# Moving ScalarE's weight casts and slice stores, and one VectorE shift, in a hand-ordered attention block

## The chip, the cores and the metric

The program runs on one core of a Trainium2 chip. The metric is the device time of one execution in microseconds (us). It is compared as the median of several executions; the kernel before had 2206.11 us as the median of three (2204.46 to 2212.1).

## What is computed

A two-layer block on 64 sequences of 32 tokens with 512 features (2048 tokens), all in float32. Only the first layer's attention is touched by the change:

```python
x = x + L0_attn(L0_cond(x, ...), wq, wkv, wo)     # 32 heads of 128, softmax over 32 keys, causal
x = x + L0_ffn(L0_cond2(x, ...), ...)
x = x + L1_attn(L1_cond(x, ...), ...)
x = x + L1_ffn(L1_cond2(x, ...), ...)

# L0_attn
q = einsum('bsd,de->bse', h, wq);  k, v = the two halves of einsum('bsd,de->bse', h, wkv)
probs = softmax(where(causal, q @ k.T * scale, -1e30))
return einsum('bse,ed->bsd', probs @ v, wo)
```

## The kernel before

The first layer's attention is one block of the program (function `attention`), from about 88 to 1686 us of the profiled span. Every engine has its own list of instructions there, written out by hand, and the lists meet only in semaphores. No scheduler decides anything: the order in the source is the order on each engine.

**Bodies and slots.** The 2048 tokens are two pairs of tiles of 512 tokens (`pair` 0 and 1), and the 32 heads are eight groups of four. One `body(it, pair, ...)` does four heads for one pair of tiles; there are sixteen of them, `it` 0 to 7 for pair 0 and 8 to 15 for pair 1. A body is six slots `s`. Slots 0, 1, 4 and 5 make queries and keys (`qk`) of one head each, slots 2 and 3 the values (`v_tok`) of all four. Each slot's product of weights and input is done with seven smaller products instead of eight (`product`, names P1 to P7), where weights and inputs were combined by sums first. Each float32 product is three TensorE matmuls on a high and a low part (`mm3`, lines 215 to 217).

**Weights.** `HeadWeights` prepares the seven combined weight blocks `j` of a slot. ScalarE writes the high part (`high`, line 984: a cast), GpSimd forms the four sums (`sums`: lines 997, 1000, 1003 and 1007) and subtracts for the low part (`low`, line 1018). The weights of a slot are called H0, H1, V (slots 2 and 3 together), H2 and H3. The high part `(1,)` has to wait for GpSimd's second sum (line 1000), and GpSimd's first sum (line 997) writes to a place that TensorE's product P5 of the slot before still reads:

```python
if j in SUM_OF:
    act.wait_ge(self.sum_done, w * 4 + (SUM_OF[j] + 1))
act.activation(self.part(kind, j, 0), src, ACT.Copy).then_inc(self.hi_done, 1)
```

**Copies.** In a slot, three products leave PSUM by ScalarE's `copy_chain(it, s, k)` (line 1250; k = 0, 1, 2 behind P6, P5 and P3), one by `keep_p1` (line 1242), and three by VectorE's `mix(it, s, k)` (line 1421; behind P2, P7 and P4). TensorE's P5 waits for `copy_chain(.., 0)`, and its P3 for `copy_chain(.., 1)`.

**Softmax and output.** `scores` (line 1708) is followed on VectorE by `soft_shift` (lines 1438, 1443, 1444), on ScalarE by `exps` (line 1255), on VectorE by `soft_divide` (1451 to 1453) and `soft_turn` (1459, four transposes of 32x32 blocks). `prob_times_v` (line 1719) is followed by ScalarE's `o_high` (line 1260, two casts of 128x512 to `o_hi`) and VectorE's `o_low` (line 1465, two subtractions to `o_lo`). Then `output(T, m)`, four times six matmuls with `wo`, waits in its first call for both low parts:

```python
if m == 0:
    pe.wait_ge(wo_ready, ow + 1)
    pe.wait_ge(tail_free, T * 6 + 5)
```

The results are added to the residual by VectorE's `add_out` (line 1471).

**Slices for the second pair.** During pair 0, VectorE's `part(j)` (lines 1401, 1406, 1408) forms a slice of the combined inputs of the second half of the tokens in `stage`, and ScalarE's `store(j)` (line 1236) sends it to DRAM by DMA. `stage` is one buffer, so each `part` waits until the store before has landed. In pair 1 `store` and `part` do nothing. `out_high` (line 1273) casts the 128x1024 output weights.

Of the kernel before, what the change touches and what calls it, by code (L numbers as in the profile page):

```python
# [1050 lines left out]
def attention(nc, t, sb, sem, overlaid, const, consts, mm3, resid, psum, kept_raw, kept, hw, v_tok, combos, later, ahead):  # L1051
# [7 lines left out]
    with ctx:  # L1059
# [172 lines left out]
        @block.scalar  # L1232
        def _(act):
            def store_part(it, j):
                wait_apart(act, part_step, parts_done(it, PART_ORDER.index(j) + 1), hw.passed)
                act.dma_start(y_parts[j][:, :, :, slice_of(it)], stage[:].bitcast(F32)).then_inc(part_out, 16)

            def keep_p1(it, s, first=False):
                g = it * SETS + s
                act.wait_ge(prod_done, product_count(g, 0))  # L1240
                act.wait_ge(mix_done, g * 3 + 1)
                act.activation(p1, psum[:, bank_of(s, 0, first), :], ACT.Copy).then_inc(p1_done, 1)

            def copy_chain(it, s, k, first=False):
                g = it * SETS + s
                j = (1, 2, 6)[k]
                act.wait_ge(prod_done, product_count(g, j))
                if k == 0 and s in (0, 1, 5) and not (first and s == 0):
                    act.wait_ge(scores_done, it * 4 + {0: 1, 1: 2, 5: 4}[s])
                act.activation(destination(s, (1, 1, 0)[k], (0, 1, 1)[k]), psum[:, bank_of(s, j, first), :],  # L1250
                               ACT.Copy).then_inc(chain_copied, 1)

            def exps(sm):
                act.wait_ge(shifted, sm + 1)
                act.activation(ex[:], sc[:], ACT.Exp).then_inc(exp_done, 1)

            def o_high(T):
                for a in range(GH):
                    act.wait_ge(pv_done, T * GH + (a + 1))
                    act.activation(o_hi[:, a, :], psum[:, 5 + a, :], ACT.Copy).then_inc(o_hi_done, 1)  # L1260

            def end_exps(i):
                act.wait_ge(shifted, END + i + 1)
                act.activation(ex[:, half(i), :], sc[:, half(i), :], ACT.Exp).then_inc(exp_done, 1)

            def end_high(i):
                for a in range(GH):
                    act.wait_ge(pv_done, (END + i) * GH + (a + 1))
                    act.activation(end_o_hi[i][:, a, :], psum[:, END_BANKS[i] + a, :], ACT.Copy).then_inc(o_hi_done, 1)

            def out_high(ow, wo_raw=wo_raw, wo=wo):
                act.wait_ge(o_in, ow * 16 + 16)
                act.activation(wo[:, 0, :], wo_raw[:, 1, :], ACT.Copy).then_inc(wo_hi_done, 1)

            def body(it, pair, first=False, turn=False, turned=False, last=False):
                def store(j):
                    if pair == 0:
                        store_part(it, j)

                hw.high(act, it, "H1", (0,))  # L1280
                store(0)
                copy_chain(it, 0, 0, first)
                hw.high(act, it, "H1", (1,))
                copy_chain(it, 0, 1, first)
                if not first:
                    exps(it * 4)
                hw.high(act, it, "H1", (2, 3))
                keep_p1(it, 1)
                hw.high(act, it, "H1", (4,))
                copy_chain(it, 0, 2, first)  # L1290
                hw.high(act, it, "H1", (5, 6))
                if not first:
                    out_high(it * 2)

                hw.high(act, it, "V", (0,), fresh=first)
                copy_chain(it, 1, 0)
                if not first:
                    o_high(it * 4)
                copy_chain(it, 1, 1)
                exps(it * 4 + 1)  # L1300
                hw.high(act, it, "V", (1, 2, 3), fresh=first)
                keep_p1(it, 2)
                hw.high(act, it, "V", (4,), fresh=first)
                copy_chain(it, 1, 2)
                hw.high(act, it, "V", (5, 6), fresh=first)
                if not first:
                    o_high(it * 4 + 1)

                hw.high(act, it, "H2", (0,))
                copy_chain(it, 2, 0)  # L1310
                hw.high(act, it, "H2", (1,))
                copy_chain(it, 2, 1)
                exps(it * 4 + 2)
                hw.high(act, it, "H2", (2, 3))
                keep_p1(it, 3)
                hw.high(act, it, "H2", (4,))
                copy_chain(it, 2, 2)
                hw.high(act, it, "H2", (5, 6))
                store(4)

                copy_chain(it, 3, 0)
                out_high(it * 2 + 1)
                copy_chain(it, 3, 1)
                store(3)
                keep_p1(it, 4)
                copy_chain(it, 3, 2)

                hw.high(act, it, "H3", (0,))
                copy_chain(it, 4, 0)
                hw.high(act, it, "H3", (1,))  # L1330
                o_high(it * 4 + 2)
                copy_chain(it, 4, 1)
                store(1)
                hw.high(act, it, "H3", (2, 3))
                keep_p1(it, 5)
                hw.high(act, it, "H3", (4,))
                copy_chain(it, 4, 2)
                hw.high(act, it, "H3", (5, 6))
                store(2)
                o_high(it * 4 + 3)  # L1340
                store(5)

                if not last:
                    hw.high(act, it + 1, "H0", (0,))
                copy_chain(it, 5, 0)
                if not last:
                    hw.high(act, it + 1, "H0", (1,))
                copy_chain(it, 5, 1)
                exps(it * 4 + 3)
                if last:  # L1350
                    copy_chain(it, 5, 2)
                    act.wait_ge(x1_c2_in, 16 * (KC + 1))
                    for i in range(4):
                        act.activation(kept[:, i * C2_PIECE:(i + 1) * C2_PIECE],
                                       kept_raw[:, C2_LO + i * C2_PIECE:C2_LO + (i + 1) * C2_PIECE],
                                       ACT.Copy).then_inc(c2_hi_done, 1)
                else:
                    hw.high(act, it + 1, "H0", (2, 3))
                    store(6)
                    keep_p1(it + 1, 0)  # L1360
                    hw.high(act, it + 1, "H0", (4,))
                    copy_chain(it, 5, 2)
                    hw.high(act, it + 1, "H0", (5, 6))

            act.sem_inc(chain_copied, 3)
            act.sem_inc(exp_done, 1)
            act.sem_inc(o_hi_done, 4)
            act.sem_inc(wo_hi_done, 1)
            for j in range(1, 7):
                if j in (1, 4, 5):  # L1370
                    act.wait_ge(late_sum, {1: 1, 5: 2, 4: 3}[j])
                act.activation(first_y.place(j, 0, LATE), first_y.source(j, LATE), ACT.Copy).then_inc(late_hi, 1)
            keep_p1(0, 0, True)
            quads(act, body)
            out_high(4 * QUADS, last_wo_raw, last_wo)
            for i in range(2):
                end_exps(i)
            for i in range(2):
                end_high(i)
            for c in range(KC):  # L1380
                act.activation(ahead[0][:, c, :], resid[:, c, 0:TT], ACT.Copy).then_inc(late_hi, 1)

        @block.vector
        def _(dve):
# [77 lines left out]
            def o_low(T):  # L1462
                for a in range(GH):
                    dve.wait_ge(o_hi_done, T * GH + (a + 1))
                    dve.tensor_tensor(o_lo[:, a, :], psum[:, 5 + a, :], o_hi[:, a, :].bitcast(F32),  # L1465
                                      ALU.subtract).then_inc(tail_free, 1)
# [6 lines left out]
            def body(it, pair, first=False, turn=False, turned=False, last=False):  # L1473
                before = 0 if turned else pair
                sm, T = it * 4, it * 4
# [13 lines left out]
                mix(it, 0, 2)  # L1489

                mix(it, 1, 0)
                soft_shift(sm + 1)
                if not first:
                    o_low(T)
                mix(it, 1, 1)
                soft_divide(sm + 1)
                if not first:
# [53 lines left out]
                if not last:  # L1551
                    add_out(T + 3, 2, pair, 1)
                    add_out(T + 3, 3, pair, 1)
                soft_turn(sm + 3, 0, it * 8 + 8)
                mix(it, 5, 2)

            dve.sem_inc(mix_done, 3)
            dve.sem_inc(soft_step, NSOFT)
# [1451 lines left out]
```

## Time and profile before

| | us |
|---|---|
| runs | 2204.46, 2206.11, 2212.1; median 2206.11 |
| the profiled execution | 2203.17 |
| its span | 2201.3 |
| TensorE matmul busy | 2120.5 (96%) |
| GpSimd, VectorE, ScalarE busy | 1016.5, 1250.5, 817.4 |
| mean granted TensorE clock | 0.994 of full speed |

TensorE is busy nearly everywhere, and the other engines are busy about half the time. A row of the timeline gives the start (us), the duration (us), the engine, the source line, the operation, output and input, and the count; in brackets stands the idle time before it and what ended it.

### The profile page before, as it was taken

What the parts mean: (1) busy time and instruction counts of PE and PEld (TensorE: products, weight loads), DVE (VectorE), ACT (ScalarE), POOL (GpSimd) and SP (SyncE); (2) the same over time, 40 slices, a digit from 0 to 9 for tenths busy, and PEclk for the clock granted to TensorE, in tenths of its full rate; (3) what the DMA queues carried; (4) which work ended last, traced back from release to release, by engine and by line L of the source; (5) the groups of instructions that cost most, each with busy time, mean ns of one, the idle gap of its engine ahead of it and who ended that gap; (6) DMA issues with size and microseconds to landing.
All of it is one profiled execution on the core that took longest, in us unless ns stands there. A gap on an engine that the chain in (4) does not pass through costs nothing. (4 is left out here: it accounts for less than half of the span.)

```text
span 2201.3 us, 36345 instructions
## 1 busy us (share of the span) xinstructions
PE 2120.5 (96%) x11922; PEld 1824.1 (83%) x11922; DVE 1250.5 (57%) x2427; ACT 817.4 (37%) x1636; POOL 1016.5 (46%) x1123
## 2 busy tenths in 40 slices
PE   7989999999999999999999999999999999999999
PEld 5878888888888888878888888888887878878887
DVE  8646465655646565545546464545547766655444
ACT  5333232433333232433333232433333654434332
POOL 4556363645536363645536363655534752204220
PEclk9999999999999999999999999999999999999999
DMA  7511113111111115311111112111111120001110
GB/s 233 167 40 46 51 43 83 53 47 48 48 48 45 50 46 189 111 34 44 38 38 38 38 43 62 48 38 38 39 50 57 55 79 0 0 0 31 43 41 19
DMA packets 122612, 122.26 MB, mean 56 GB/s; under 512 B 35249, under 2 KB 101457, under 8 KB 120497
## 3 DMA queue, kind: packets, MB, share of 16 engines
q1 hardware_dynamic: 91697, 109.87, 16.1%
q10 hardware_dynamic: 29568, 7.34, 1.6%
q0 software_dynamic: 1280, 4.20, 0.7%
q8 instruction: 37, 0.61, 0.1%
q14 instruction: 30, 0.25, 0.0%
HBM read 108.13 MB, written 13.28 MB: 55 GB/s over the span
## 5 line engine op out<-in xcount | busy, mean ns | idle before, releaser
L215 PE MATMUL psum<-yc,wh 128*128 128x512 f32 x904 | 364.5, 403 | 2.8 <-ACT qk L1250 1.3
L216 PE MATMUL psum<-yc,wh 128*128 128x512 f32 x904 | 353.8, 391 | 0.0
L217 PE MATMUL psum<-yc,wh 128*128 128x512 f32 x904 | 353.3, 391 | 0.0
L1471 DVE TENSOR_TENSOR resid<-psum,resid 128x512 f32<-128x512 f32 x248 | 169.8, 690 | 196.8 <-PE psum L217 190.9
L1018 POOL TENSOR_TENSOR wh<-wh_f,wh 128x256 fp32r<-128x256 f32 x256 | 187.6, 736 | 186.1 <-ACT wh L984 180.1
L1018 POOL TENSOR_TENSOR wh<-raw,wh 128x256 fp32r<-128x256 f32 x192 | 148.1, 771 | 266.1 <-ACT wh L984 265.3
L215 PE MATMUL psum<-kept,yc 128*128 128x256 f32 x896 | 256.8, 287 | 5.8 <-ACT v_tok L1250 3.1
L216 PE MATMUL psum<-kept,yc 128*128 128x256 f32 x896 | 253.8, 283 | 0.0
L217 PE MATMUL psum<-kept,yc 128*128 128x256 f32 x896 | 253.8, 283 | 0.0
L215 PE MATMUL psum<-o_hi,wo 128*128 128x512 f32 x496 | 200.4, 404 | 45.5 <-DVE o_lo L1465 31.9
L984 ACT ACTIVATE wh<-wh_f 128x256 fp32r<-128x256 f32 x256 | 105.0, 410 | 279.1 <-POOL wh_f L1000 249.0
L215 PEld LDWEIGHTS psum<-yc,wh 128*128 128x128 f32 x904 | 171.6, 190 | 40.6 <-issue 4.4
L217 PEld LDWEIGHTS psum<-yc,wh 128*128 128x128 f32 x904 | 170.3, 188 | 36.2
L216 PE MATMUL psum<-o_lo,wo 128*128 128x512 f32 x496 | 197.3, 398 | 0.0
L216 PEld LDWEIGHTS psum<-yc,wh 128*128 128x128 f32 x904 | 171.5, 190 | 30.7
L217 PE MATMUL psum<-o_hi,wo 128*128 128x512 f32 x496 | 196.5, 396 | 0.0
L215 PEld LDWEIGHTS psum<-kept,yc 128*128 128x128 f32 x896 | 171.6, 192 | 11.5 <-ACT v_tok L1250 4.7
L216 PEld LDWEIGHTS psum<-kept,yc 128*128 128x128 f32 x896 | 171.8, 192 | 3.6
L1250 ACT ACTIVATE qk<-psum 128x512 f32<-128x512 f32 x192 | 113.7, 592 | 157.6 <-PE psum L217 92.6
L217 PEld LDWEIGHTS psum<-kept,yc 128*128 128x128 f32 x896 | 171.6, 192 | 0.0
L215 PEld LDWEIGHTS psum<-o_hi,wo 128*128 128x128 f32 x496 | 95.1, 192 | 70.0 <-DVE o_lo L1465 36.9
L997 POOL TENSOR_TENSOR wh_f<-raw 128x256 f32<-128x256 f32 x64 | 47.3, 739 | 214.3 <-PE psum L217 214.3
(363 smaller groups left out, 4577.9 us busy)
## 6 DMA issues: line engine op xcount, KB each, us to landing
raw<-in_attn_w SPq DMA_DIRECT2D x96, 512.0 KB, 5.0
wo_f<-in_attn_w SPq DMA_DIRECT2D x31, 512.0 KB, 4.0
hankel<-kernel_rows SPq DMA_DIRECT2D x32, 256.0 KB, 4.8
y_parts<-stage ACTq DMA_DIRECT2D x56, 128.0 KB, 2.3
yc<-y_parts SPq DMA_DIRECT2D x7, 1024.0 KB, 5.1
resid<-in_xT SPq DMA_DIRECT2D x4, 1024.0 KB, 9.7
outT<-wide SPq DMA_DIRECT2D x16, 256.0 KB, 2.6
kept_f<-in_l_w SPq DMA_DIRECT2D x3, 1024.0 KB, 5.5
```

Of the source, the lines that this page charges most:

```text
L215: pe.matmul(out, w[0], x[0], start=start, stop=False, skip_group_check=onto)
L216: pe.matmul(out, w[0], x[1], start=False, stop=False, skip_group_check=onto)
L217: return pe.matmul(out, w[1], x[0], start=False, stop=stop, skip_group_check=onto)
L984: act.activation(self.part(kind, j, 0), src, ACT.Copy).then_inc(self.hi_done, 1)
L997: pool.tensor_tensor(s1, a21, a22, ALU.add).then_inc(self.sum_done, 1)
L1018: pool.tensor_tensor(self.part(kind, j, 1), src, self.part(kind, j, 0).bitcast(F32), ALU.subtract).then_inc(self.lo_done, 1)
L1250: act.activation(destination(s, (1, 1, 0)[k], (0, 1, 1)[k]), psum[:, bank_of(s, j, first), :], ACT.Copy).then_inc(chain_copied, 1)
L1471: dve.tensor_tensor(part, psum[:, 5 + (GH + m) % 3, :], part, ALU.add).then_inc(tail_free, 1)
```

## The change

All of it is in three engine lists' order; no instruction is added or removed. On ScalarE (in `body`): in slots 0, 4 and 5 the high part `(1,)` of the next weights goes from in front of `copy_chain(.., 1)` to behind it, and so behind `exps` in slots 0 and 5, behind `o_high(it * 4 + 2)` and `store(1)` in slot 4. In slot 3, `store(4)` goes behind `copy_chain(it, 3, 0)` and `out_high` behind `copy_chain(it, 3, 1)`. On VectorE: in slot 1 `o_low(T)` goes ahead of `soft_shift(sm + 1)`, and at the end of slot 5 `soft_turn` goes behind `mix(it, 5, 2)`. TensorE's and GpSimd's orders stay.

```diff
@@ ScalarE, slot 0
                 copy_chain(it, 0, 0, first)
-                hw.high(act, it, "H1", (1,))
                 copy_chain(it, 0, 1, first)
                 if not first:
                     exps(it * 4)
-                hw.high(act, it, "H1", (2, 3))
+                hw.high(act, it, "H1", (1, 2, 3))
@@ ScalarE, slots 3 and 4
                 hw.high(act, it, "H2", (5, 6))
+
+                copy_chain(it, 3, 0)
                 store(4)
-
-                copy_chain(it, 3, 0)
+                copy_chain(it, 3, 1)
                 out_high(it * 2 + 1)
-                copy_chain(it, 3, 1)
                 store(3)
...
                 copy_chain(it, 4, 0)
-                hw.high(act, it, "H3", (1,))
                 o_high(it * 4 + 2)
                 copy_chain(it, 4, 1)
                 store(1)
-                hw.high(act, it, "H3", (2, 3))
+                hw.high(act, it, "H3", (1, 2, 3))
@@ ScalarE, slot 5
                 copy_chain(it, 5, 0)
-                if not last:
-                    hw.high(act, it + 1, "H0", (1,))
                 copy_chain(it, 5, 1)
                 exps(it * 4 + 3)
...
-                    hw.high(act, it + 1, "H0", (2, 3))
+                    hw.high(act, it + 1, "H0", (1, 2, 3))
@@ VectorE, slot 1
                 mix(it, 1, 0)
-                soft_shift(sm + 1)
                 if not first:
                     o_low(T)
+                soft_shift(sm + 1)
                 mix(it, 1, 1)
@@ VectorE, end of slot 5
+                mix(it, 5, 2)
                 soft_turn(sm + 3, 0, it * 8 + 8)
-                mix(it, 5, 2)
```

The sources' line numbers behind ScalarE's list are four lower in the changed kernel (1461 for 1465, 1417 for 1421 and so on).

ScalarE in slots 3 and 4 of the first body. L1236 is a store, L1250 a `copy_chain`, L1273 `out_high`, L1242 `keep_p1`, L984 a high part and L1260 `o_high`. Before:

```order
L1236 DMA y_parts<-stage 512x1x64
L1250 ACTIVATE v_tok<-psum 128x512
L1273 ACTIVATE wo<-wo_f 128x1024
L1250 ACTIVATE v_tok<-psum 128x512
L1236 DMA y_parts<-stage 512x1x64
L1242 ACTIVATE kept_f<-psum 128x512
L1250 ACTIVATE v_tok<-psum 128x512
L984 ACTIVATE wh<-raw 128x256
L1250 ACTIVATE qk<-psum 128x512
L984 ACTIVATE wh<-wh_f 128x256
L1260 ACTIVATE o_hi<-psum 128x512 x2
L1250 ACTIVATE qk<-psum 128x512
```

And now:

```order
L1250 ACTIVATE v_tok<-psum 128x512
L1236 DMA y_parts<-stage 512x1x64
L1250 ACTIVATE v_tok<-psum 128x512
L1273 ACTIVATE wo<-wo_f 128x1024
L1236 DMA y_parts<-stage 512x1x64
L1242 ACTIVATE kept_f<-psum 128x512
L1250 ACTIVATE v_tok<-psum 128x512
L984 ACTIVATE wh<-raw 128x256
L1250 ACTIVATE qk<-psum 128x512
L1260 ACTIVATE o_hi<-psum 128x512 x2
L1250 ACTIVATE qk<-psum 128x512
L1236 DMA y_parts<-stage 512x1x64
```

The first copy of slot 3 now stands in front of the store, and the cast of `wh_f` no longer stands in front of the two casts to `o_hi`.

VectorE at the end of slot 5 and the start of the next body's slot 0 (the branch is the loop's; L1421 is `mix`, L1459 `soft_turn`, L1406 and L1408 are `part(0)`). Before:

```order
L1471 TENSOR_TENSOR resid<-psum,resid 128x512 x2
L1459 STREAM_TRANSPOSE probT<-ex 32x8x32 x4
L1421 TENSOR_TENSOR qk<-psum,qk 128x512
L1104 UNCONDITIONAL_BRANCH
L1104 ISA
L1406 ISA
L1406 COPY stage<-resid 128x128
L1407 ISA
L1408 TENSOR_TENSOR stage<-resid,stage 128x128
```

And now, where the same lines are numbered four lower:

```order
L1467 TENSOR_TENSOR resid<-psum,resid 128x512 x2
L1417 TENSOR_TENSOR qk<-psum,qk 128x512
L1455 STREAM_TRANSPOSE probT<-ex 32x8x32 x4
L1104 UNCONDITIONAL_BRANCH
L1104 ISA
L1402 ISA
L1402 COPY stage<-resid 128x128
L1403 ISA
L1404 TENSOR_TENSOR stage<-resid,stage 128x128
```

The four transposes now stand between the last `mix` of the body and the `part(0)` of the next.

VectorE in slot 1 (L1438, L1443 and L1444 are `soft_shift`, L1465 is `o_low`). Before:

```order
L1421 TENSOR_TENSOR qk<-psum,kept_f 128x512
L1434 REGISTER_ALU
L1438 SCALAR_TENSOR_TENSOR sc<-psum,consts 32x256 x4
L1429 ISA
L1443 TENSOR_REDUCE stat<-sc 128x8
L1429 REGISTER_ALU
L1444 TENSOR_TENSOR sc<-sc,stat 128x256
L1464 ISA
L1465 TENSOR_TENSOR o_lo<-psum,o_hi 128x512
L1464 REGISTER_ALU
L1465 TENSOR_TENSOR o_lo<-psum,o_hi 128x512
```

And now:

```order
L1417 TENSOR_TENSOR qk<-psum,kept_f 128x512
L1460 ISA
L1461 TENSOR_TENSOR o_lo<-psum,o_hi 128x512
L1460 REGISTER_ALU
L1461 TENSOR_TENSOR o_lo<-psum,o_hi 128x512
L1430 REGISTER_ALU
L1434 SCALAR_TENSOR_TENSOR sc<-psum,consts 32x256 x4
L1425 ISA
L1439 TENSOR_REDUCE stat<-sc 128x8
L1425 REGISTER_ALU
L1440 TENSOR_TENSOR sc<-sc,stat 128x256
```

The two low parts now stand in front of the shift's six instructions.

## Rows read from the trace of the kernel before

**Rows 1.** The page: busy time of the engines.

```profile
PE 2120.5 (96%) x11922; PEld 1824.1 (83%) x11922; DVE 1250.5 (57%) x2427; ACT 817.4 (37%) x1636; POOL 1016.5 (46%) x1123
```

**Rows 2.** Who waited for whom, TensorE: us in total, times, longest us.

```profile
PE psum L215 <- DVE o_lo L1465: 31.9, 12, 2.7
PE psum L215 <- issue: 11.0, 4, 2.8
...
PE psum L215 <- ACT v_tok L1250: 3.1, 7, 1.3
...
PE psum L1708 <- DVE qk L1421: 1.0, 5, 0.3
```

**Rows 3.** Timeline of TensorE, slot 4 of bodies 1 and 3.

```profile
250.85 0.79 PE L215 MATMUL psum<-o_hi,wo 128*128 128x512 f32 x1 [2.66 <-DVE o_lo L1465]
...
446.47 0.39 PE L217 MATMUL psum<-yc,wh 128*128 128x512 f32 x1
449.51 0.49 PE L215 MATMUL psum<-o_hi,wo 128*128 128x512 f32 x1 [2.66 <-DVE o_lo L1465]
```

**Rows 4.** Windows of TensorE: us, busy (x), granted clock, DMA share, GB/s.

```profile
943.40:946.60 3.20, 3.20 (x8) 0.50 0.00 0
449.50:452.70 3.20, 3.19 (x14) 1.00 0.02 5
```

**Rows 5.** Timelines of ScalarE, VectorE and GpSimd, slot 4 of body 3.

```profile
447.16 0.42 ACT L984 ACTIVATE wh<-wh_f 128x256 fp32r<-128x256 f32 x1 [5.55 <-POOL wh_f L1000]
447.49 0.58 ACT L1260 ACTIVATE o_hi<-psum 128x512 fp32r<-128x512 f32 x1
...
448.10 1.29 DVE L1465 TENSOR_TENSOR o_lo<-psum,o_hi 128x512 fp32r<-128x512 f32 x2 [4.94 <-ACT o_hi L1260]
...
445.58 0.74 POOL L997 TENSOR_TENSOR wh_f<-raw 128x256 f32<-128x256 f32 x1 [5.68 <-PE psum L217]
```

**Rows 6.** Timeline, `prob_times_v` and `o_high`: TensorE in slots 4 and 1, then ScalarE in slot 1.

```profile
442.18 1.95 PE L1719 MATMUL psum<-probT,v_tok 128*128 128x128 f32 x16
...
494.12 1.95 PE L1719 MATMUL psum<-probT,v_tok 128*128 128x128 f32 x16
...
496.10 0.60 ACT L1260 ACTIVATE o_hi<-psum 128x512 fp32r<-128x512 f32 x1 [0.30 <-PE psum L1719]
```

**Rows 7.** Timeline, slot 3: ScalarE's first copy behind the store, and TensorE.

```profile
530.20 0.60 ACT L1250 ACTIVATE v_tok<-psum 128x512 f32<-128x512 f32 x1 [4.07 <-DVE stage L1408]
...
530.85 0.39 PE L215 MATMUL psum<-kept,yc 128*128 128x256 f32 x1 [0.27 <-ACT v_tok L1250]
```

**Rows 8.** Timeline, end of slot 5 and slot 0 of body 4: VectorE, ScalarE, TensorE.

```profile
474.22 0.29 DVE L1408 TENSOR_TENSOR stage<-resid,stage 128x128 fp32r<-128x128 f32 x1
...
475.80 1.78 DVE L1459 STREAM_TRANSPOSE probT<-ex 32x256 f32<-32x256 f32 x4
478.00 0.69 DVE L1421 TENSOR_TENSOR qk<-psum,qk 128x512 f32<-128x512 f32 x1 [0.42 <-PE psum L217]
478.71 0.52 DVE L1406 CAST stage<-resid 128x128 fp32r x1
479.26 0.71 DVE L1408 TENSOR_TENSOR stage<-resid,stage 128x128 fp32r<-128x128 f32 x1
...
480.32 0.55 ACTq L1236 DMA_DIRECT2D y_parts<-stage  x1
481.05 0.60 ACT L1250 ACTIVATE qk<-psum 128x512 f32<-128x512 f32 x1 [2.11 <-PE psum L1708]
...
482.23 0.39 PE L215 MATMUL psum<-yc,wh 128*128 128x512 f32 x1
```

**Rows 9.** Timeline, slot 1 of body 4: VectorE, GpSimd, then slot 2's first product on TensorE.

```profile
495.01 1.71 DVE L1438 SCALAR_TENSOR_TENSOR sc<-psum,consts 32x256 f32<-32x256 f32 x4
...
499.87 2.56 POOL L1018 TENSOR_TENSOR kept<-kept_f,kept 128x512 fp32r<-128x512 f32 x2
...
510.08 0.36 PE L215 MATMUL psum<-kept,yc 128*128 128x256 f32 x1
```

## The prediction

> **What bounds the kernel now.** I first read the page's busy times: TensorE's matmuls are busy 96% of the span, the other engines half of it [rows 1]. So only two things can shorten this kernel: fewer matmuls, which the change doesn't bring, or fewer and shorter waits of TensorE. I then read who waited for whom, on TensorE alone. The reader should see that one wait stands out, that of the line-215 matmul for VectorE's `o_lo`: 31.9 us in 12 times of 2.66, and 11.0 us in 4 times of 2.75 with no releaser named [rows 2]. The timeline shows that these are one place. The sixteen stand one in each body, at the first `output` of slot 4; two of them are in [rows 3]. Together 42.9 us.
>
> Then I followed that wait back in body 3 [rows 5]. TensorE started at 449.51, right when VectorE's two low parts (448.10 to 449.39) were done. They had idled 4.94 us for ScalarE's `o_hi`, which started at 447.49 with no idle of its own: in front of it on ScalarE stood the cast of H3's high part (1,), started at 447.16 after 5.55 us of idle for GpSimd's second sum. And GpSimd had idled 5.68 us for TensorE's P5 before it began the first sum at 445.58. The `prob_times_v` whose results `o_hi` casts had started at 442.18 [rows 6]. So the results lay ready while ScalarE waited for weights that slot 5 needs.
>
> **The change, part by part.** All in-order lists; nothing is added, so each part is worth the wait that it moves.
>
> *Slot 4, the (1,) cast behind `o_high`.* In slot 1 nothing stands between: `prob_times_v` starts at 494.12 and the second `o_hi` at 496.10, 1.98 later [rows 6]. The same distance here puts the second `o_hi` at 444.16. VectorE's low part followed its `o_hi` by 0.61 us (447.49 to 448.10) and two take 1.29 [rows 5], so the second ends at 444.16 + 0.61 + 0.65 = 445.4. TensorE's last matmul of P7 starts at 446.47 [rows 3], and a dense stream has one each 0.23 us (14 in 3.20 us, [rows 4]), so it asks for them at 446.70. The low parts are then 1.3 us ahead of it, and the wait goes entirely. The cast itself waits as before for the sum (447.16), so nothing behind it gets later; `store(1)` now is in front of it, one DMA issue of 0.55 us, in time that was idle. What returns:
> - the recorded idle, 42.9 us;
> - what the row does not count. From 446.47 to 449.51 are 3.04 us, 2.81 more than the cadence of 0.23, against 2.66 recorded: 0.15. The first matmul behind takes 0.49 instead of 0.39: 0.10. Sixteen times 0.25 is 4.0;
> - the clock. In six of the sixteen the first matmul behind the wait takes 0.77 to 0.79, as at 250.85 [rows 3]; in such a stretch the granted clock is 0.50, that is 1.2 GHz, and 8 matmuls fit into 3.20 us, where in a body without that it is 1.00 (2.4 GHz) and 14 fit [rows 4]. 6 x 0.23 = 1.4 each, six times 8.2 us. I take it as returned, since in the attention block these stretches begin at this wait alone.
>
> Sum 55.1. The Trainium skill, "TensorE: Matmul & The Clock Gate", in its table "Why this matters for your kernels", warns only of idle gaps longer than each of these; by that page the slow stretches would have another cause, and the gain would be without the 8.2. The rows stand against the page here.
>
> *Slot 3, `store(4)` behind the first copy.* ScalarE's copy started at 530.20 after 4.07 us of idle for VectorE's slice, and TensorE's P5 at 530.85, 0.05 behind its end [rows 7]. In pair 0 that is 3.1 us in 7 times [rows 2], the longest 1.3. Each with the same 0.25 beside: 4.9. All goes, since the copy's own input, P6, is 1.4 us (P2's twelve matmuls of 0.12) older than P5. `store(4)` still leaves when the slice is ready, and `out_high` moves about 2.4 us back, to behind the second copy; GpSimd's `out_low` with it. Its user is `output` in slot 4, over 10 us on: nothing.
>
> *Slots 0 and 5, the (1,) cast behind copy and `exps`.* `copy_chain(.., 1)`, `exps` and all of VectorE's softmax behind them come 0.5 us (slot 0) to 2 us (slot 5) earlier. The cast waits for the same sum as before, and at slot 0 at most 0.7 us longer, for `exps`. VectorE's last `mix` of slot 0 comes earlier with it, and that was what the second `scores` of five bodies of pair 1 waited for: 1.0 us [rows 2]. I count 1.0.
>
> *VectorE, `soft_turn` behind `mix(5, 2)`.* This is the part that costs. Before, the four transposes (475.80 to 477.58) lay in idle time, and the `mix` came at once when P4 was done, at 478.00 [rows 8]. Now they start at 478.69 and end at 480.47, and only then come the two instructions of `part(0)`, for which `store(0)` waits, which stands in front of slot 0's first copy. The two took 1.26 us at 478.71, and the subtraction of a slice 0.29 instead of 0.71 at 474.22, so I take 0.55 for both. Then, as in the rows, 0.35 to the DMA issue, 0.73 to the copy, 0.60 for it: 480.47 + 0.55 + 0.35 + 0.73 + 0.60 = 482.70. TensorE's P5 starts at 482.23 [rows 8]. It will wait 0.47 + 0.05, and its first matmul 0.10: 0.6 us, in bodies 1 to 7 (pair 1 has no slices): 4.3 us. Bounds: 1.26 for the two gives 1.3 each, 9.3; if VectorE or ScalarE run ahead of this, 0.
>
> *VectorE, `o_low` ahead of the shift in slot 1.* The second `o_hi` starts at 496.10 [rows 6], so the low parts end at 496.10 + 0.61 + 0.65 = 497.36, and the shift starts there instead of at 495.01 [rows 9]: 2.35 us later. Behind it wait `exps`, and behind that on ScalarE's list the casts V(1,), V(2,), V(3,), for which GpSimd's low parts wait, from 499.87 on [rows 9]. The first of these is needed by slot 2's P6 at 510.08 [rows 9], and is done at 499.87 + 1.28 = 501.2: 8.9 us of cover against a slip of 2.4. I cost it at nothing. If the cover were gone, it would be 2.35 us in 15 bodies, 35 us; the low parts' own user, slot 1's `output`, shows no wait now, so there is no gain either.
>
> **The sum.** 55.1 + 4.9 + 1.0 - 4.3 = 56.7 us. The profiled execution had 2203.17 us; 2203.2 - 56.7 = 2146.5. The median of the runs is 2.9 above that execution, so for the median of new runs I say 2149.5.
>
> **The rivals.**
> 1. *The clock's share stays.* Slow stretches come from somewhere else and stay at 8.2 us: 2149.5 + 8.2 = 2158. For it speaks the page above and that ten waits of the same length have no slow stretch; against it that the six begin exactly at the wait. 0.10.
> 2. *The later shift in slot 1 is not covered,* through GpSimd's series of V low parts into slot 2, or VectorE's slices cost more than I count. Up to 2.35 x 15 = 35 us: from 2155 to 2185. For it: GpSimd is in that stretch without idle, so a slip is passed on. Against it: 8.9 us of cover. 0.13.
> 3. *It doesn't do what it says:* ScalarE's `o_hi` in slot 4 is held by something other than the cast. Then only slot 3's 4.9 and 1.0 come, less 4.3: 2204.5, no change. Against it: no idle between the cast and `o_hi` [rows 5]. 0.02.
> 4. *Slower than before.* The same slip as in 2 grows as GpSimd and ScalarE wait for each other in turn (V(4,) waits for GpSimd's fourth sum, and the third copy of slot 1 stands behind it). It decides from the point at which the slip is over 8.9 us; it costs 15 times what is above, and takes back all of the 56.7 at 8.9 + 3.8 = 12.7 us. With 15 us it would be 2149.5 + 91 = 2241. The first slip is 2.4, and I see nothing that makes it five times as large. 0.02.
>
> **How the numbers follow.** My forecast has 0.73. Its own range goes from 2142 (slot 0 costs nothing, and the runs lie where the profiled execution does) to 2155 (slot 0 at its upper bound). The whole range takes in rival 1 and the lower half of rival 2: 2141 to 2168. A difference under 0.3% (6.6 us) can't be told from none for this kernel. Faster by more than that are the forecast and rivals 1 and 2: 0.96; within it rival 3: 0.02; slower rival 4: 0.02.
>
> **What would show it.** TensorE's list of waits has no row for `o_lo` of 2.66 us any more; ScalarE's `o_hi` in slot 4 starts about 1.1 and 2.0 us behind `prob_times_v`; a body takes 2.9 us less, and those with a slow stretch 1.4 less again; the copy of slot 3 has no idle for the slice. New is a row of some 0.5 us, seven times, for ScalarE's `qk` copy in slot 0 of pair 0. I am wrong if a wait of over 1 us stands in every body at slot 1 or 2, or if windows behind slot 4 still show the clock at 0.50.

## The result

The changed kernel takes 2151.44 us (median of four, 2150.49 to 2152.26), the kernel before beside it 2207.38 us. The ratio is 0.9744, 95% interval 0.9726 to 0.9763: 2.6% faster. The forecast was 2149.5 in a range of 2141 to 2168.

| us | before | after |
|---|---|---|
| profiled execution | 2203.17 | 2150.74 |
| its span | 2201.3 | 2148.8 |
| TensorE matmul busy | 2120.5 | 2103.6 |
| mean granted clock | 0.994 | 0.999 |

TensorE's list of waits in the changed kernel, which answers to [rows 2] (us in total, times, longest us):

```profile
PE psum L215 <- DVE v_tok L1417: 6.9, 8, 0.9
PE psum L215 <- ACT qk L1250: 6.2, 8, 3.0
...
PE psum L1704 <- ACT qk L1250: 3.0, 9, 0.9
PE psum L215 <- DVE resid L1467: 2.6, 1, 2.6
```

The 42.9 us for `o_lo` are gone, and so are the 3.1 us for the copy of slot 3 and the 1.0 us for VectorE at the scores. Two of these rows are new: 6.9 us for VectorE's `v_tok` and 3.0 us for ScalarE at the second scores. Of the row of 6.2, the first body has 1.23 and 2.97, which the kernel before had too (3.9 in 2 times); the other 2.0 are new, and lie in slot 0 of pair 0.

Slot 4 of body 4 in the changed kernel, by the timelines of TensorE, ScalarE and VectorE, answers to [rows 3, 5, 6]:

```profile
529.98 1.95 PE L1715 MATMUL psum<-probT,v_tok 128*128 128x128 f32 x16
...
534.50 0.39 PE L215 MATMUL psum<-o_hi,wo 128*128 128x512 f32 x1
...
531.07 0.60 ACT L1260 ACTIVATE o_hi<-psum 128x512 fp32r<-128x512 f32 x1 [1.65 <-PE psum L1715]
531.96 0.60 ACT L1260 ACTIVATE o_hi<-psum 128x512 fp32r<-128x512 f32 x1 [0.30 <-PE psum L1715]
533.34 0.60 ACT L1250 ACTIVATE qk<-psum 128x512 f32<-128x512 f32 x1 [0.78 <-PE psum L217]
...
534.97 0.73 ACT L984 ACTIVATE wh<-wh_f 128x256 fp32r<-128x256 f32 x2 [1.04 <-POOL wh_f L1000]
...
532.59 0.69 DVE L1461 TENSOR_TENSOR o_lo<-psum,o_hi 128x512 fp32r<-128x512 f32 x1 [0.20 <-ACT o_hi L1260]
```

The two `o_hi` start 1.09 and 1.98 us behind `prob_times_v`, the second `o_lo` ends at 533.28, and TensorE comes for it at 534.50 with no idle. The cast still waits for GpSimd's sum, now with nobody behind it who is in a hurry.

The new wait, in slot 3 of the same body: VectorE, GpSimd, ScalarE, TensorE. It answers to [rows 7].

```profile
523.56 1.15 DVE L1402 CAST stage<-resid 128x128 fp32r x1 [3.29 <-DMA y_parts<-stage]
524.75 0.29 DVE L1404 TENSOR_TENSOR stage<-resid,stage 128x128 fp32r<-128x128 f32 x1
524.95 0.68 DVE L1417 TENSOR_TENSOR v_tok<-psum,v_tok 128x512 f32<-128x512 f32 x1
...
522.23 2.40 POOL L1187 TENSOR_TENSOR wo<-wo_f,wo 128x1024 fp32r<-128x1024 f32 x1 [6.36 <-ACT wo L1273]
...
518.09 0.55 ACTq L1236 DMA_DIRECT2D y_parts<-stage  x1
...
525.69 0.39 PE L215 MATMUL psum<-kept,yc 128*128 128x256 f32 x1 [0.86 <-DVE v_tok L1417]
```

`store(4)` was issued at 518.09. VectorE waited for its landing until 523.56, and then its cast of the next slice took 1.15 us, until 524.71, while GpSimd's subtraction of the output weights ran until 524.63. Behind the cast stands `mix(3, 1)`, for which TensorE's P4 waits. It is so in all eight bodies of pair 0: the cast takes between 0.44 and 1.73 us, always ends 0.08 us behind GpSimd's subtraction, and TensorE's wait is 0.86 us each time, though the store landed between 4.6 and 5.9 us behind its issue.

### The profile page after: what moved, and what is told of

The parts are those of the page before. It is cut to its first block and busy times, and to the rows that moved or that the text cites. A ratio compares the mean times of both kernels' runs of the same rounds, so it can differ in the third digit from the quotient of the medians.

```text
span 2148.8 us, 36345 instructions
## 1 busy us (share of the span) xinstructions
PE 2103.6 (98%) x11922; PEld 1817.5 (85%) x11922; DVE 1262.4 (59%) x2427; ACT 827.7 (39%) x1636; POOL 1013.9 (47%) x1123
## 5 line engine op out<-in xcount | busy, mean ns | idle before, releaser
L1018 POOL TENSOR_TENSOR wh<-raw,wh 128x256 fp32r<-128x256 f32 x192 | 142.2, 741 | 218.6 <-ACT wh L984 217.4
L1250 ACT ACTIVATE qk<-psum 128x512 f32<-128x512 f32 x192 | 114.4, 596 | 251.6 <-PE psum L217 185.9
L215 PE MATMUL psum<-o_hi,wo 128*128 128x512 f32 x496 | 194.5, 392 | 2.6 <-DVE resid L1467 2.6
L217 PE MATMUL psum<-o_hi,wo 128*128 128x512 f32 x496 | 193.4, 390 | 0.0
L1417 DVE TENSOR_TENSOR qk<-psum,qk 128x512 f32<-128x512 f32 x128 | 88.5, 692 | 89.3 <-PE psum L217 87.8
L984 ACT ACTIVATE wh<-wh_f 128x256 fp32r<-128x256 f32 x256 | 100.0, 408 | 98.3 <-POOL wh_f L1000 52.2
```

What stands on the lines that cost most here:

```text
L215: pe.matmul(out, w[0], x[0], start=start, stop=False, skip_group_check=onto)
L217: return pe.matmul(out, w[1], x[0], start=False, stop=stop, skip_group_check=onto)
L1018: pool.tensor_tensor(self.part(kind, j, 1), src, self.part(kind, j, 0).bitcast(F32), ALU.subtract).then_inc(self.lo_done, 1)
L1417: dve.tensor_tensor(out, psum[:, product_bank(s, j), :], p1 if k == 0 else out, ALU.add).then_inc(mix_done, 1)
```

## The experiments

The rows are those of one execution, and the median of a kernel's runs can lie up to 4 us from it (4.2 for the kernel before, 3.7 for e2). Where a few microseconds matter I read a second measure from TensorE's timeline: the attention block from the wait of 1.2 us near 95 us (ScalarE's `qk` in the first body) to the wait of 0.30 us for `PEq L264` in the last body. Both stand in every run.

| kernel | median us | ratio to before (95%) | block, us |
|---|---|---|---|
| before | 2207.38 | | 1561.1 |
| changed | 2151.44 | 0.9744 (0.9726 to 0.9763) | 1507.9 |
| e1 slot 4 alone | 2148.28 | 0.9733 (0.9709 to 0.9756) | 1504.5 |
| e2 all but slot 4 | 2216.09 | 1.0040 (1.0028 to 1.0052) | 1576.0 |
| e3 turn back | 2149.57 | 0.9742 (0.9720 to 0.9763) | 1505.9 |
| e4 out_high back | 2147.30 | 0.9726 (0.9705 to 0.9747) | 1503.2 |
| e5 exps behind cast | 2149.49 | 0.9740 (0.9726 to 0.9753) | 1506.9 |
| e6 o_low back | 2152.11 | 0.9756 (0.9742 to 0.9770) | 1509.8 |
| e7 e3, e4 and e5 | 2140.58 | 0.9699 (0.9685 to 0.9713) | 1498.1 |
| e8 shift later | 2154.20 | 0.9761 (0.9745 to 0.9777) | 1512.1 |
| e9 e7, part(3) behind | 2138.71 | 0.9689 (0.9676 to 0.9702) | 1497.1 |
| e10 e9, third copies | 2132.37 | 0.9664 (0.9651 to 0.9677) | 1487.6 |

One thing has to be taken out of the blocks. Behind the first body's wait of some 3 us near 118 us, TensorE's clock was half in the profiled executions of e1 and e3 to e9 (a granted clock of 0.57 to 0.69 over the 4 us behind the wait), for longer in that of e2 (0.50 over those 4 us), and full in those of before, changed and e10. Such a stretch costs about 1.4 us. Against the changed kernel, e1 and e3 to e9 are therefore 1.4 us shorter in what the edits do than the table's blocks say.

### Slot 4 by itself

```diff
                 copy_chain(it, 4, 0)
-                hw.high(act, it, "H3", (1,))
                 o_high(it * 4 + 2)
                 copy_chain(it, 4, 1)
                 store(1)
-                hw.high(act, it, "H3", (2, 3))
+                hw.high(act, it, "H3", (1, 2, 3))
```

> The kernel before with one edit: in slot 4 the cast H3 (1,) stands behind o_high, the second copy and store(1). Theory A (slot 4 is the whole gain, the rest of the change gives and takes in equal parts): the sixteen waits of 2.7 us and the six slow stretches go, 2203.2 - 55.1 = 2148 us in a profiled execution, 2148 to 2151 as a median, so the same as the whole change or 2 us better; the waits of 0.27 us in slot 3 stay, and no wait of TensorE for VectorE's v_tok appears. Theory B (the other parts are needed, because the 2.8 us gained in slot 4 would be lost at slot 1's output, where the low parts were only just in time): a wait of 1 us or more per body at slot 1, 2165 us or more. Clock: by A the mean granted clock is 0.999, as in the changed kernel.

Measured: 2148.28 us; the profiled executions are 2203.17 and 2147.99, 55.2 apart, where the prediction had 55.1 for this part. By the medians it is 58.5 (2206.74 for the kernel before beside it), by the block 56.6, and 58.0 without the first body's stretch at half clock. So the part is worth 55 to 58 us, and the agreement to 0.1 is luck. TensorE's waits in this kernel:

```profile
PE psum L215 <- ACT v_tok L1250: 2.3, 7, 0.5
PE psum L1707 <- DVE qk L1420: 1.1, 6, 0.3
```

Theory A holds. One moved cast is the whole gain, and the version with only this is some 3 us faster than the whole change: 3.2 by the medians (the intervals overlap), 3.4 by the block and 4.8 without the first body's stretch. Where the rest of the change loses, a body's length tells: in pair 0 it is 95.73 us here (421.43 to 517.16) and 96.63 in the changed kernel (470.93 to 567.56), in pair 1 95.33 (1145.78 to 1241.11) and 95.06 (1151.10 to 1246.16). So the other parts cost in pair 0 and give a little in pair 1. Compared matmul by matmul, the 0.90 us of that body of pair 0 are 0.57 lost at slot 0's P5, 0.28 won in slots 0 and 1, and in slot 3 0.54 won and 1.13 lost. Slot 1's output did not become the next wait.

### Everything but slot 4

The same two pieces of code exchanged the other way in the changed kernel.

> The changed kernel with slot 4 of ScalarE put back as it was: every part of the change but that one. Theory A: the sixteen waits for o_lo of 2.7 us are back, 2150.7 + 55.1 = 2206 us, so within 0.3% of the kernel before (2207). If the slow stretches belong to this wait, then 5 to 8 of the 16 bodies show the granted clock at 0.50 behind it again and the mean clock is 0.994; if they had another cause, the clock stays at 0.999 and the time is about 2198. Theory B: the other parts carry half of the gain, 2180 us.

Measured: 2216.09 us, 0.4% slower than before, where 2206 was expected, within 0.3% of before, with 5 to 8 stretches at half clock and a mean clock of 0.994. The wait is back, 42.9 us to the tenth, and so is the clock's loss, with more of it:

```profile
PE psum L215 <- DVE o_lo L1462: 31.9, 12, 2.7
PE psum L215 <- issue: 11.0, 4, 2.8
...
PE psum L215 <- DVE v_tok L1418: 7.6, 8, 1.5
PE psum L215 <- ACT qk L1250: 6.2, 8, 3.0
...
PE psum L1705 <- ACT qk L1250: 3.0, 9, 1.0
```

Windows of TensorE behind that wait in two bodies of this kernel (us, busy (x), granted clock, DMA share, GB/s):

```profile
855.80:862.00 6.20, 6.12 (x15) 0.50 0.01 3
...
1057.00:1060.00 3.00, 3.00 (x7) 0.50 0.01 3
```

Stretches at half clock stand behind the wait in 10 of 16 bodies, more than expected; in one it held for 6.2 us. The mean clock is 0.989. In e1 no body has one in slot 4; the only two of that kernel are behind the first body's wait of 2.68 us and behind the one at the block's end. Taken away and put back, the wait takes the stretches with it. Theory B falls: the other parts together cost time with slot 4 (3 us by the medians) and without it, though here part of the 9 us is the clock. This profiled execution has eleven stretches at half clock in the block, two of them (behind the first body's wait and at 855.80) twice as long as the others, against seven before. Six times 1.4 us more is 8.4 of the 14.9 us between the blocks, which leaves 6.5 us for the parts; both are estimates.

### The part that was to cost: soft_turn

```diff
-                mix(it, 5, 2)
                 soft_turn(sm + 3, 0, it * 8 + 8)
+                mix(it, 5, 2)
```

> The changed kernel with soft_turn ahead of mix(5, 2) again. The wait of TensorE for ScalarE's qk copy in slot 0 of pair 0 (0.48 once, 0.30 five times, each 0.46 to 0.64 against the cadence plus a longer first matmul) goes: 6 x 0.6 + 0.3 = 4 us less than the changed kernel, 2147. Rival (the two instructions of part(0) collide with GpSimd's last low part of H0 when they come early, as in the kernel before, and the store is no earlier): the wait stays and the time is 2151.

Measured: 2149.57 us, the block 2.1 shorter. The wait at slot 0's P5 is gone, but a part of it comes again six products later, at the second scores:

```profile
PE psum L1704 <- ACT qk L1250: 4.3, 15, 0.9
PE psum L215 <- ACT qk L1250: 4.2, 2, 2.9
```

The row of the second scores went from 9 times to 15, the new ones 0.2 us each in pair 0. They look larger than they are: in the changed kernel the same matmul was 0.27 us late too (0.50 us behind the one before it, where 0.23 is the cadence), which is an idle too short for the list; with e3's edit it is 0.37. So some 0.1 of the 0.57 us at P5 comes again. A body of pair 0 is 96.12 us (478.29 to 574.41) instead of 96.63, seven times 0.5, so 3.5 of the 4 expected. The block shows only 2.1 of it, since this is one of the executions with the half clock behind the first body's wait (TensorE between 119 and 123 us):

```profile
119.00:123.00 4.00, 4.00 (x26) 0.67 0.02 7
```

In the changed kernel that window has 34 matmuls at 1.00. The medians alone, 1.9 apart, don't tell this kernel from the changed one; the rows do.

### The collision in slot 3

```diff
                 copy_chain(it, 3, 0)
                 store(4)
+                out_high(it * 2 + 1)
                 copy_chain(it, 3, 1)
-                out_high(it * 2 + 1)
```

> The changed kernel with out_high ahead of the second copy of slot 3 again (store(4) still behind the first copy). Theory C: the eight new waits of 0.86 us in slot 3 come from a collision: out_high late makes GpSimd's 128x1024 subtraction (2.40 us from 522.23) lie over VectorE's cast of part(3) at 523.56, which takes 1.15 us instead of 0.23; with out_high early GpSimd is done before the slice has landed, the cast takes 0.23, and the wait is 0 to 0.1: 8 x 1.1 = 8 us less, 2142. Theory D: they come from the landing of store(4) alone, since TensorE now reaches P4 0.4 us earlier: the cast would start at the same time and the wait would only shrink by what the cast is shorter if that is what counts; if the landing is what counts, 0.5 us or more per body stay and the time is 2147 or more.

Measured: 2147.30 us, 4.1 less than the changed kernel and not 8. VectorE, then GpSimd, in the same slot:

```profile
522.30 0.23 DVE L1402 CAST stage<-resid 128x128 fp32r x1 [3.56 <-DMA y_parts<-stage]
...
518.85 2.40 POOL L1187 TENSOR_TENSOR wo<-wo_f,wo 128x1024 fp32r<-128x1024 f32 x1 [4.51 <-ACT wo L1273]
```

```profile
PE psum L215 <- DVE v_tok L1417: 1.3, 4, 0.7
```

With GpSimd done at 521.25, the cast takes 0.23 us as by theory C, and the row shrinks from 6.9 to 1.3 us in 4 times. These four are theory D's share: in those bodies `store(4)` landed 5.3 to 5.8 us behind its issue, in the other four 4.9 to 5.15. The block is 4.7 shorter, 6.1 without the first body's stretch.

### The cast ahead of exps

```diff
                 copy_chain(it, 0, 1, first)
+                hw.high(act, it, "H1", (1,))
                 if not first:
                     exps(it * 4)
-                hw.high(act, it, "H1", (1, 2, 3))
+                hw.high(act, it, "H1", (2, 3))
```

> The changed kernel with the cast H1 (1,) of slot 0 behind the copy but ahead of exps. Theory E: the waits of TensorE for ScalarE's qk copy at the second scores (3.0 us recorded in 9 times, against 1.0 for VectorE before) come from this cast: behind exps it starts late, GpSimd's low parts and fourth sum slip by what it is later, and the cast (4,) and the third copy of slot 0 with them. With the cast ahead of exps these waits go, 15 bodies x 0.2 to 0.35 = 3 to 4 us less: 2147. Rival: the slip comes from GpSimd's own start (its first sum waits for P5, which comes at the same time in both), the waits stay, 2151.

Measured: 2149.49 us. The row of the second scores for ScalarE is gone, as theory E has it; one wait of 0.50 us for VectorE stands in body 9. But the row's end isn't the wait's: in body 11 the first matmul of the scores came 0.69 us behind the one before it in the changed kernel and comes 0.50 behind it here. What is left is too short for the list; e10, below, takes it away. The gain is 2.0 us by the medians and 2.4 by the block without the first body's stretch, where 3 to 4 were expected. In pair 0 the wait at slot 0 stays at 6.2 in 8 times.

### o_low

```diff
-                if not first:
-                    o_low(T)
                 soft_shift(sm + 1)
+                if not first:
+                    o_low(T)
```

> The changed kernel with o_low behind the shift in slot 1 again. Prediction's theory: this part is worth nothing in either direction: 2150.7 within 0.1%, no wait of TensorE in slot 1 or 2. Rival: before, the low parts of slot 1 ended 0.1 us ahead of the output; with the slip at slot 0 gone or changed they come late now, a wait for o_lo at slot 1's first output of 0.1 to 0.5 us in 15 bodies, 2153 to 2158.

Measured: 2152.11 us, 0.7 more by the median; 1.9 by the block, of which the first body's stretch is 1.4. No new wait for `o_lo` appears in the list. About 0.5 us is left, of which 0.3 is a longer wait for `v_tok` in the first body (1.14 for 0.86): nothing, as predicted, or just above.

### How much cover the shift has

```diff
-                soft_shift(sm + 1)
                 mix(it, 1, 1)
+                soft_shift(sm + 1)
```

> The changed kernel with the shift of slot 1 moved one step further, behind mix(1, 1), which measures the cover that the prediction put at 8.9 us. The shift slips by another 3.7 us (from 486.0 to 489.7 in body 4). By the prediction's reasoning (cover 8.9 us, through GpSimd's low parts of V) nothing waits and the time stays at 2151. Rival: the cover is VectorE's own list, where the first residual addition of slot 1 ends at 492.5 and TensorE asks for it at 495.6: 3.0 us; then TensorE waits 0.5 to 1.5 us in 15 bodies at the fourth output of slot 1 or at the third scores, 2158 to 2175.

Measured: 2154.20 us, 2.8 more. One row of the list has grown from 0.8 us in 1 time:

```profile
PE psum L215 <- ACT kept_f L1242: 2.5, 2, 1.7
```

The new 1.7 us are in the first body, at 116.36, where no `o_low` stands in front and GpSimd has just started on V. The other 15 bodies keep their length but for one (0.26 us longer, between slot 4 of bodies 1 and 2): from 277.69 to 664.16 us it is 386.5 in the changed kernel, from 281.74 to 668.22 in this one 386.5 too. But the shift slipped less than the edit was to give: in body 4 it starts at 492.26, where the changed kernel's 485.98, moved by the 4.05 us that this kernel lies behind, would be 490.03. That is 2.2 us, with the change's own 2.35 about 4.6 against before; and VectorE's first residual addition behind it comes at 497.73, 1.8 us later than 491.85 + 4.05. So a slip of 4.6 us of the shift is covered in 14 of these 15 bodies, and costs 0.26 us in one. The rival with 3.0 us of cover on VectorE's list is not decided, since the slip there stayed below it, and neither are the 8.9 us that the prediction counted.

### The three together

> The changed kernel with the edits of three runs together: soft_turn ahead of mix(5, 2), out_high ahead of the second copy of slot 3, the cast H1 (1,) ahead of exps in slot 0. If the three waits are independent: 2150.7 - 4 - 8 - 3.5 = 2135 us, and TensorE's waits in the attention block are only those of the first body and of the block's end. If they hide one another (TensorE arriving earlier at the next late thing), 2139 to 2143.

Measured: 2140.58 us, 10.9 less than the changed kernel, where 15.5 was the sum and the second range 8 to 12.

```profile
PE psum L215 <- ACT qk L1250: 4.2, 2, 3.0
...
PE psum L215 <- DVE v_tok L1418: 2.6, 5, 0.9
```

e3's waits at the scores are not in this list. By the medians the three edits give 1.9, 4.1 and 2.0 us singly, 8.0 in all, and 10.9 together. By the block, with the first body's stretch taken out, they give 3.5, 6.1 and 2.5 singly, 12.1 in all, and 11.2 together. So they add up, as far as these measures tell, and neither that they hide one another nor that they gain from being together is shown; 15.5 was too much because the sizes expected for e4 and e5 were. The kernel beats both kernels and e1 (7.7 us).

### Two more places

```diff
                 mix(it, 3, 0)
-                part(3)
                 mix(it, 3, 1)
+                part(3)
```

> The kernel of e7 with VectorE's part(3) behind mix(3, 1). What is left of the wait in slot 3 (2.6 us in 5 of 8 bodies, 0.21 to 0.90) is put down to the landing of store(4): part(3) waits for it in front of the mix that TensorE's P4 waits for. With the mix in front, P4 no longer depends on the DMA: all five waits go, 2.6 + 5 x 0.2 = 3.5 us less than e7 (2140.6), 2137, and no row of TensorE waiting for v_tok from VectorE is left. Rival (the mix itself is late, behind TensorE's P7 and ScalarE's copy): 0.2 us or more per body stay and the time is 2140.

Measured: 2138.71 us. The row for `v_tok` is gone, as expected, but part of it moved one step on, to the copy that stands behind `store(3)` on ScalarE (0.8 us of this row, at 92.69, stand in every kernel; 0.52 and 1.11 are new):

```profile
PE psum L215 <- ACT kept_f L1242: 2.4, 3, 1.1
```

In those two bodies `store(4)` landed 6.3 and 6.9 us behind its issue, in the other six 4.9 to 5.9. So the landing still reaches TensorE in single bodies, by `part(3)`, `store(3)` and `keep_p1(4)`. The gain of 1.9 us is within what the runs of one kernel differ (2136.5 to 2141.75); I don't call it shown.

```diff
+                copy_chain(it, 0, 2, first)
                 hw.high(act, it, "H1", (4,))
-                copy_chain(it, 0, 2, first)
...
+                copy_chain(it, 1, 2)
                 hw.high(act, it, "V", (4,), fresh=first)
-                copy_chain(it, 1, 2)
```

> The kernel of e9 with the same lesson applied at two more places: ScalarE's third copy of slots 0 and 1 ahead of the casts H1 (4,) and V (4,), which wait for GpSimd's fourth sum. Expected: the wait of 2.97 us in the first body, and the stretch at half clock (1.4 us) that stands behind it in some executions, go, and the wait of 0.49 us at body 9's second scores gets shorter or stays: 3 to 4.5 us less than e9, 2133. Rival: in the first body the third copy is late for another reason (TensorE's P3 waits for GpSimd's V low parts), the wait moves to a row with GpSimd or VectorE as its releaser, and the time is that of e9.

Measured: 2132.37 us (2130.92 to 2133.06), 3.4% less than before and 19.1 us less than the changed kernel. The 2.97 us in the first body are gone, and three short waits stand in their place:

```profile
115.96 0.39 PE L215 MATMUL psum<-kept,yc 128*128 128x256 f32 x1 [0.50 <-POOL kept L1018]
...
119.79 0.36 PE L215 MATMUL psum<-kept,yc 128*128 128x256 f32 x1 [0.34 <-ACT v_tok L1250]
...
125.07 0.35 PE L215 MATMUL psum<-kept,yc 128*128 128x256 f32 x1 [0.74 <-ACT v_tok L1250]
```

The gain on e9 is 6.3 us by the medians and 9.5 by the block, more than the wait and the stretch at half clock behind it (4.4 at most); e9's two new waits for `kept_f`, 1.6 us, are not in this one either. The rest is a wait that no list showed. TensorE at the second scores of body 11, in e9 and then in this kernel:

```profile
1236.03 0.39 PE L217 MATMUL psum<-yc,wh 128*128 128x512 f32 x1
1236.53 0.68 PE L1705 MATMUL psum<-qk 128*128 128x128 f32 x4
```

```profile
1226.55 0.39 PE L217 MATMUL psum<-yc,wh 128*128 128x512 f32 x1
1226.78 0.72 PE L1705 MATMUL psum<-qk 128*128 128x128 f32 x5
```

In e9 the scores come 0.50 us behind the matmul before them, just when slot 0's third copy is done (1236.38), and here 0.23, the cadence. With the second matmul's 0.08 that is 0.35 us in that body and 0.26 in body 4, so 4 to 5 us over the block. In bodies 1 to 14 one wait of TensorE is listed in this kernel, 0.49 us.

## Why the prediction was right, point by point

**What bounds the kernel.** Right. TensorE's waits were the only thing worth moving, and the one place named was the whole gain.

**Slot 4.** Right in mechanism and size. The wait goes entirely, `o_hi` and `o_lo` come at the predicted distances, and e1 measures 55 to 58 us, by the measure taken, for a term of 55.1. Its third part, the clock, was rightly put down to the wait, as e1 and e2 show by taking it away and putting it back. It was counted a little low, at six stretches: a seventh is in the first body, where the half clock begins 1 us behind the wait and so doesn't show in the first matmul (TensorE in the kernel before):

```profile
151.40:154.20 2.80, 2.80 (x8) 0.50 0.00 0
```

**The page of the Trainium skill** ("TensorE: Matmul & The Clock Gate", "Why this matters for your kernels") warns of longer gaps only. The waits here are 2.66 to 2.75 us, and half clock stood behind 7 of 16 before and 10 of 16 in e2. The measurement decides: gaps of this length cost clock too, about every second time. Rival 1 falls.

**Slot 3.** The step that failed: "`store(4)` still leaves when the slice is ready, and `out_high` moves about 2.4 us back ...: nothing". The first half is true, the old wait went (3.1 us to none), but a new one of 6.9 us in 8 times came. I asked only who uses the output weights, and not on which instructions of VectorE GpSimd's 2.40 us would now lie. In the changed kernel the collision sets the end of the cast in all eight bodies; e4, which takes it away, leaves 1.3 us in four of them for the landing of the store. The term was +4.9 and is about -4.

**Slots 0 and 5.** Wrong in mechanism: +1.0 was counted because the wait at the second scores would go, and the row went from 1.0 to 3.0. I had seen that the cast gets at most 0.7 us later behind `exps` and left it at that; GpSimd's fourth sum and the third copy slip with it, and they had no cover left. e5 takes the row away. The term as a whole did not lose time, though: in pair 1, where no slice is made, the same four bodies take 381.31 us in e1 (1050.45 to 1431.76) and 380.25 in the changed kernel (1056.04 to 1436.29). In body 11, P3 of slot 0, which waits for `copy_chain(0, 1)`, came 0.19 us late in e1 and is on time now, and slot 1's first output gained 0.1; the prediction had priced neither, so that +1.0 has the right sign is luck.

**soft_turn.** Right in mechanism and size. In body 4 of the changed kernel the last matmul before P5, of P2, starts at 470.24, so P5 was due at 470.47, and it came at 470.93:

```profile
470.24 0.39 PE L217 MATMUL psum<-yc,wh 128*128 128x512 f32 x1
470.93 0.50 PE L215 MATMUL psum<-yc,wh 128*128 128x512 f32 x1 [0.30 <-ACT qk L1250]
```

That is 0.46, and 0.10 in the first matmul: 0.56 against 0.6. The wait recorded is 0.30 us in five bodies and 0.48 in one, so over the seven some 3.8 us against 4.3. The two instructions of `part(0)` took 0.55 us as assumed (468.65 to 469.20). e3 gets 3.5 of it back.

**o_low and the shift.** Right: nothing, as e6 shows. Rivals 2 and 4 would have needed a slip to reach TensorE; e8's 4.6 us don't, but for 0.26 us in one body and the wait in the first. How much more is covered stays open. In the first body the cover is not there; the prediction had not looked at it.

**The sum.** 56.7 was forecast, 52.4 is what the two profiled executions differ by. The three smaller terms (+4.9, +1.0, -4.3) were to give 1.6 together, and against e1 they took 3 to 5 (3.2 by the medians, 3.4 by the block, 4.8 without e1's stretch in the first body). That the median came out within 1.9 us of the forecast is in part luck: 2.9 us were added from the profiled execution to the median, as in the kernel before, and it was 0.7.

## What to carry to other kernels

On an engine whose list is in order, ask of each instruction that waits whether a result with an earlier deadline lies ready behind it; here one cast of 0.4 us, whose weights are asked for more than 10 us later, held 2.8 us of TensorE in every body. When a wait is removed, look at what runs beside each moved instruction as well as at who uses it: a long GpSimd subtraction moved by 2 us cost more than the wait it came with. Try the parts of a change singly: the best single move beat the whole. And compare the distance of matmuls with their cadence, since a wait that has left the list needn't be gone: 0.3 us in each body stood in no list, and came to 4 or 5.

## What the runs showed that I had not expected

GpSimd and VectorE hold each other up at single instructions. VectorE's 128x128 cast takes 0.23 us alone; begun while GpSimd's 128x1024 subtraction is under way, it ends 0.08 us behind that one in all eight bodies, after 0.44 to 1.73 us. Only the overlap was shown; by what path they collide was not tried.

The clock falls behind a wait of the same length in some executions and not in others. The wait of 2.6 us at the end of the block is followed by 1.00 in the kernel before, and by 0.50 in the changed one:

```profile
1615.90:1618.30 2.40, 2.40 (x7) 0.50 0.00 0
```

So one such wait is worth 2.8 us, or 1.4 more, and two profiled executions of nearly the same kernel can differ by that; a row tells, a total doesn't.
